# Softmax sums of two attentions in four column groups of the tensor engine, reciprocals spread by DMA

## The reference

```python
logits = einsum('bqhgd,bkhd->bhgqk', qg, k) * scale      # layer 0: 4 key heads, rotary
w = softmax(where(causal, logits, -1e30), axis=-1)
out = einsum('bhgqk,bkhd->bqhgd', w, v)                  # layer 1: the same with 16 key heads
```

## Time and profile before

| what | value |
|---|---|
| median of 3 runs | 1986.06 us (1983.82 to 1986.65) |
| time of the profiled execution | 1981.67 us |
| its span, first to last instruction | 1979.9 us |
| busy: PE / DVE / ACT / POOL | 1832.5 / 1336.2 / 958.2 / 1239.3 us |
| attention of layer 0, about | 45 to 529 us of the span |
| attention of layer 1, about | 690 to 1150 us of the span |
| mean granted clock of TensorE | 0.967 |
| DMA | 155.96 MB, 134304 packets on SP's queue |

### The profile page before, as it was taken

The page is one execution under the profiler, slowest core; times in us unless marked ns, Lnnn a source line. Parts: engine busy times, 40 slices in busy tenths (PEclk is TensorE's granted clock), DMA queues, the critical chain, the costliest instruction groups (busy, mean ns, idle before and its releaser), DMA issues.

```text
span 1979.9 us, 31923 instructions
## 1 busy us (share of the span) xinstructions
PE 1832.5 (93%) x10080; PEld 1273.4 (64%) x10080; DVE 1336.2 (67%) x3765; ACT 958.2 (48%) x2008; POOL 1239.3 (63%) x1454
## 2 busy tenths in 40 slices
PE   5999999999896899999999999999889999988985
PEld 4566666666595566676766567787556666655564
DVE  8899888888344866666667446556677787764633
ACT  2544445455455455554555534546344545544543
POOL 1766788888654467767777710011367888789953
PEclk8999999999998899999999999999789999999997
DMA  5224243232153343543444220000313233323243
GB/s 151 68 66 114 65 104 92 71 70 62 48 180 92 89 102 76 117 93 86 102 95 98 66 89 22 1 13 1 85 41 72 61 72 78 71 67 85 62 126 97
DMA packets 138569, 155.96 MB, mean 79 GB/s; under 512 B 34480, under 2 KB 78800, under 8 KB 138144
## 3 DMA queue, kind: packets, MB, share of 16 engines
q1 hardware_dynamic: 134304, 145.80, 30.0%
q0 software_dynamic: 4096, 8.12, 1.3%
HBM read 47.96 MB, written 17.52 MB: 33 GB/s over the span
## 4 chain that ended last, share of the span: by engine, by line
PE 61%; DVE 13%; POOL 10%; issue 6%; ACT 3%; SPq 3%; DMA 3%; POOLq 0%; DVEq 0%; ACTq 0%
PE P L904 60%; POOL acc L1707 3%; POOL yd L1730 3%; DVE mx L2118 3%; SPq L1834 2%; DMA qA<-hq 2%; DVE P L2129 2%; POOL xg L1721 1%; POOL acc L1704 1%; POOL pr L1685 1%; ACT pr L1450 1%; PE P L1003 1%; POOL z L1713 1%; PE P L942 0%; DVE mx L2129 0%
## 5 line engine op out<-in xcount | busy, mean ns | idle before, releaser
L1707 POOL TENSOR_TENSOR acc<-acc,pr 128x512 f32<-128x512 f32 (+5 forms) x640 | 659.8, 1050 | 43.1 <-ACT pr L1450 18.2
L1450 ACT ACTIVATE pr<-P 128x512 f32<-128x512 f32 (+1 forms) x768 | 396.8, 568 | 327.9 <-PE P L904 285.1
L904 PE MATMUL P<-pr,vt 128*64 128x512 f32 (+3 forms) x2304 | 403.4, 491 | 5.0 <-POOL pr L1685 4.8
L904 PE MATMUL P<-qA,kA 128*128 128x512 f32 (+2 forms) x1024 | 389.1, 383 | 13.9 <-ACT pr L1450 13.1
L904 PE MATMUL P<-qB,kB 128*128 128x512 f32 (+2 forms) x1024 | 368.0, 365 | 0.0
L904 PE MATMUL P<-kA,qA 128*128 128x512 f32 (+2 forms) x1152 | 316.8, 377 | 32.8 <-DMA qA<-hq 11.5
L1685 POOL TENSOR_SCALAR_AFFINE_SELECT pr<-pr 128x256 f32<-128x256 f32 x384 | 156.7, 409 | 277.1 <-ACT pr L1450 218.4
L904 PEld LDWEIGHTS P<-pr,vt 128*64 128x64 f32 x2304 | 154.4, 137 | 226.3 <-issue 189.7
L2118 DVE TENSOR_REDUCE mx<-P 128x1 f32<-128x512 f32 x384 | 243.7, 684 | 35.9 <-PE P L904 33.8
L904 PEld LDWEIGHTS P<-kA,qA 128*128 128x128 f32 x1152 | 193.9, 196 | 98.6 <-issue 24.3
L904 PEld LDWEIGHTS P<-qA,kA 128*128 128x128 f32 x1024 | 195.1, 191 | 90.9 <-ACT pr L1450 45.6
(11 more groups left out here) (355 smaller groups left out, 2842.0 us busy)
## 6 DMA issues: line engine op xcount, KB each, us to landing
qA<-hq SPq DMA_DIRECT2D x384, 128.0 KB, 2.4
kA<-stage SPq DMA_DIRECT2D x158, 128.0 KB
qB<-qB SPq DMA_DIRECT2D x96, 128.0 KB, 2.4
kB<-stage SPq DMA_DIRECT2D x79, 128.0 KB
rb<-sum_share SPq DMA_DIRECT2D x60, 128.0 KB, 2.9
yd<-in_c_zero SPq DMA_DIRECT2D x32, 128.0 KB, 2.7
w<-in_L_W SPq DMA_DIRECT2D x16, 256.0 KB, 5.0
xg<-xg SPq DMA_DIRECT2D x24, 129.0 KB
```

The lines of the kernel that those rows point to most:

```text
L904: return P.matmul(out, lhs, rhs, start=start, stop=stop)
L1450: S.activation(a.pr[slot][:, r, 512 - wide:512], m.bank[b][:, 512 - wide:512], AF.Exp, scale=0.125).then_inc(s.free[b], 1)
L1707: G.tensor_tensor(acc[:, :, sl], acc[:, :, sl], pt[:, :, sl], ALU.add).then_inc(s.acc, 1)
```

## The change

In layers 0 and 1:

- `C` is four matmuls of 32 output columns over 256 queries: group g (rows 32g to 32g+31) holds head g // 2, queries 256 (g % 2) and on.
- `yinv` works on 128 x 256 and no longer waits for the D of the chunk before but for its widening transfers.
- A new step `N` (newt, VectorE): the Newton step on 128 x 256, two instructions; it frees the bank of the sum.
- A new step `Y` (widen, SP): waits for N, for the widening transfers of the chunk before and for the output projection that read `z` last; then it issues four DMAs, each of which copies one row of `rd` (1 KB) onto 64 rows of `z`.
- `D` is one instruction, `z = pv * z` on 128 x 512; it waits for the four transfers.
- The orders of layers 0 and 1 are written anew.

```diff
-                if kind in HELD and len(got) == n - 1 and (kind != "close" or at_once(*item[1:4])):
-                    self.held[b] = (HELD[kind],) + item[1:]
+                    self.held[b] = ("newt" if kind == "close" and item[1] != 3 else HELD[kind],) + item[1:]
...
 STEPS = {
-    0: ("k0 S q0 k0' R1 S q1 q0' S S C1 k0\" q1' q0\" D1 q1\" V1 k1 + S M2 S M0 k1' S v1 M4 + S M1 C0 V + k1\" + "
-        "D0 R0 M6 S + M5 O0 M8 S v0 O1 M3 S S M7 V2 + + M9"),
-    1: ("S + + q0 q0' S k0 R1 k0' S S + q1 k0\" C1 q0\" D1 q1' + q1\" V1 S v0 S M1 M0 S O1 v1 M2 + S M5 M3 + S + "
-        "k1' k1 M6 S C0 + V1 k1\" + R0 D0 + M4 S M7 + S + V4 M8 O0 M9 + +"),
+    0: ("k0 S q0 k0' R1 S q1 q0' S C1 S V1 k0\" N1 Y1 q1' q0\" q1\" k1 M2 + S D1 M0 k1' S v1 S + M4 S M1 C0 V + k1\" + N0 Y0 R0 M6 S M5 + D0 M8 S O0 v0 O1 M3 S S M7 V2 + + M9"),
+    1: ("S + q0' q0 + S k0 R1 k0' S S q1 k0\" C1 q0\" N1 Y1 + q1' + q1\" V1 S M0 v0 M1 D1 S S O1 M2 v1 + S M5 M3 + S + k1' k1 M6 C0 + k1\" S V1 + + Y0 R0 N0 M4 S M7 D0 V4 + S + M8 O0 M9 +"),
...
+        elif kind in ("newt", "widen"):
+            if L != 3:
+                od.add(kind, *done)
...
-                if at_once(*k[0:3]):
+                if L == 3 and at_once(*k[0:3]):
                     for r in range(2):
                         t = mm(ps[64 * r:64 * r + 64, :], m.ones[:], acc[:, r, :], True, True)
...
-                if old and at_once(*old[0:3]):
+                if old and L != 3:
+                    w.wait_ge(s.widen, 64 * od.nth("widen", *old))
+                elif old and at_once(*old[0:3]):
...
-                own.mark(S.activation(a.rd[:], m.bank[b][:], AF.Ln))
+                cols = slice(0, 512 if L == 3 else 256)
+                own.mark(S.activation(a.rd[:, cols], m.bank[b][:, cols], AF.Ln))
                 own.settle()
-                S.activation(a.rd[:], a.rd[:], AF.Exp, scale=-1.0).then_inc(s.inv, 1)
+                S.activation(a.rd[:, cols], a.rd[:, cols], AF.Exp, scale=-1.0).then_inc(s.inv, 1)
...
+            elif kind == "widen":
+                a, old = m.A[k[0]], pl.put_out(*k)
+                z = a.z[pl.chunk(*k) % 4]
+                w.wait_ge(*pl.emptied("close", *k))
+                w.wait_ge(s.widen, 64 * od.nth("widen", *k) - 64)
+                if old:
+                    w.wait_ge(*pl.filled("out", *old))
+                for g in range(4):
+                    Y.dma_start(z[64 * (g // 2):64 * (g // 2) + 64, 256 * (g % 2):256 * (g % 2) + 256],
+                                a.rd[32 * g:32 * g + 1, 0:256].unsqueeze(1).broadcast_to([1, 64, 256])).then_inc(s.widen, 16)
...
+            elif kind == "newt":
+                y = m.A[k[0]].rd[:, 0:256]
+                b, _, _ = od.bank[("close",) + k][0]
+                sums = m.bank[b][:, 0:256]
+                w.wait_ge(s.inv, od.nth("yinv", *k))
+                chain(V.scalar_tensor_tensor(out=sums, in0=sums, scalar=-1.0, in1=y, op0=ALU.mult, op1=ALU.mult))
+                V.scalar_tensor_tensor(out=y, in0=sums, scalar=2.0, in1=y, op0=ALU.add, op1=ALU.mult).then_inc(s.free[b], 1)
+            elif kind == "div" and k[0] != 3:
+                z = m.A[k[0]].z[pl.chunk(*k) % 4]
+                b, _, _ = od.bank[("pv",) + k + (0,)][0]
+                w.wait_ge(s.pv, od.nth("pv", *k, kts(k[0], k[3])[-1]))
+                w.wait_ge(s.widen, 64 * od.nth("widen", *k))
+                V.tensor_tensor(z[:], m.bank[b][:], z[:], ALU.mult).then_inc(s.free[b], 1)
```

More of the change, by code:

```diff
@@ L201 @@
 SCORED = [(0, kt) for kt in range(4)] + [(1, kt) for kt in range(8)]
-SHARES_OUT = {"C": "close", "F": "fold", "I": "recip", "W": "spread", "B": "cast", "Z": "zraw", "D": "div", "O": "out"}
+SHARES_OUT = {"C": "close", "F": "fold", "I": "recip", "W": "spread", "B": "cast", "Z": "zraw", "N": "newt", "Y": "widen", "D": "div", "O": "out"}
 STEPS = {
-    0: ("k0 S q0 k0' R1 S q1 q0' S S C1 k0\" q1' q0\" D1 q1\" V1 k1 + S M2 S M0 k1' S v1 M4 + S M1 C0 V + k1\" + "
-        "D0 R0 M6 S + M5 O0 M8 S v0 O1 M3 S S M7 V2 + + M9"),
-    1: ("S + + q0 q0' S k0 R1 k0' S S + q1 k0\" C1 q0\" D1 q1' + q1\" V1 S v0 S M1 M0 S O1 v1 M2 + S M5 M3 + S + "
-        "k1' k1 M6 S C0 + V1 k1\" + R0 D0 + M4 S M7 + S + V4 M8 O0 M9 + +"),
-    3: ("q0 + k0' + k0 k1 q0' k0\" S V3 + R1 S q0\" + v0 C1 S S + M1 M0 F1 k1' S q1' q1 S + + W1 Z1 q1\" M2 I1 + "
-        "B1 + S v1 k1\" + V4 + M5 S O0' + D1 M3 S F0 X0 M6 C0 + R0 + W0 M4 S M9 V4 I0 Z0 + + M8 S M7 S X1 D0 "
-        "O1 B0")}
+    0: ("k0 S q0 k0' R1 S q1 q0' S C1 S V1 k0\" N1 Y1 q1' q0\" q1\" k1 M2 + S D1 M0 k1' S v1 S + M4 S M1 C0 V + k1\" + N0 Y0 R0 M6 S M5 + D0 M8 S O0 v0 O1 M3 S S M7 V2 + + M9"),
+    1: ("S + q0' q0 + S k0 R1 k0' S S q1 k0\" C1 q0\" N1 Y1 + q1' + q1\" V1 S M0 v0 M1 D1 S S O1 M2 v1 + S M5 M3 + S + k1' k1 M6 C0 + k1\" S V1 + + Y0 R0 N0 M4 S M7 D0 V4 + S + M8 O0 + M9 +"),
+    3: ("q0 + k0' + k0 k1 q0' k0\" S V3 + R1 S q0\" + v0 C1 S S + M1 M0 F1 k1' S q1' q1 S + + W1 Z1 q1\" M2 I1 + B1 + S v1 k1\" + V4 + M5 S O0' + D1 M3 S F0 X0 M6 C0 + R0 + W0 M4 S M9 V4 I0 Z0 + + M8 S M7 S X1 D0 O1 B0")}
 def project(L, kind, b, p, c):
@@ L743, in signals @@
     s.q_hi, s.k_hi, s.inv, s.recip, s.div = one("q_hi"), one("k_hi"), one("inv"), one("recip"), one("div")
-    s.fold, s.spread, s.cast = one("fold"), one("spread"), one("cast")
+    s.fold, s.spread, s.cast, s.widen = one("fold"), one("spread"), one("cast"), one("widen")
     s.rt_wh, s.rt_exp, s.xs, s.c_act, s.silu = one("rt_wh"), one("rt_exp"), one("xs"), one("c_act"), one("silu")
```

## The result

| | before | after |
|---|---|---|
| median of 3 runs | 1986.06 us | 2436.72 us (2434.48 to 2436.89) |
| span of the profiled execution | 1979.9 us | 2435.1 us |
| mean granted clock of TensorE | 0.967 | 0.897 |
| first close to last close, layer 0 | 469.9 us | 674.8 us |
| first close to last close, layer 1 | 468.2 us | 703.7 us |

The kernel is slower by 450.7 us: the ratio is 1.2288, with a 95% interval of 1.2262 to 1.2314. The last two lines of the table come from the timelines of PE, from the first to the last start of `P<-acc,ones` in a layer. Layers 0 and 1 carry 440 of the 450 us.

A forecast was written before the change was run, and what follows sets the result against it. PE's list bounds both attentions. Layer 0 +10.5, layer 1 +15, first and last jobs' closes -2, ends +5: +28.5 on the profiled 1981.67 gives 2010.2; the median lies 4.4 higher, 2014 us. Range 1968 to 2110.

The forecast's parts named there:

- The sign: Whole kernel: slower by more than the 4 us a measurement can tell, chance 0.7.
- the landing of the one-row transfers: Layers 0 and 1, Y's four copies: landing taken as 2.4 us, with 2.9 and 5.3 as other readings.
- slow rows: Rival: one-row transfers land at 5.3 us, delaying M4, M5 and D0's reader; 2143 us; chance 0.2.
- The closes: PE in layers 0 and 1: each close falls from 0.91 to 0.57 us, gaining 0.34 on each of 64.
- the odd jobs: Layer 1: Y1 adds 2.4 us before M5, less 0.34 for C0; C1's gain is lost in the wait.
- The orders: Layer 0, first half of a job: one filler outside a gap and one gap empty, +0.44 us.
- The push of q1's copies: SP's queue: Y1's four issues, 2.4 us, delay q1's copies; +10.5 us in layer 0, +15 in layer 1, closes included.
- the ends: End of each attention, last chunk uncovered: issues and landing add 4.2, shorter work saves 1.9; +2.3 twice, +5 us.
- ScalarE and VectorE: Layers 0 and 1: Ln and exp fall from 0.60 to 0.37 us, Newton from 0.70 to 0.42, covered by PE.
- D0's cover: VectorE: D0 stands late enough for its transfers; in layer 0 about 8.3 us after C0, with no wait for O0.

The follow-up runs named there:

- e9: Changed kernel in exactly the orders of before, without the widening transfers, D multiplying by other data of the same size: 1961.02 us, ratio 0.9883.
- e4: Changed kernel with its new orders, without the widening transfers, D multiplying by another tile: 2013.33 us, ratio 1.012.
- e1: Changed kernel with each widening transfer reading 32 equal rows twice instead of one row 64 times: 2065.76 us, ratio 1.0388.
- e12: Changed kernel with each widening transfer reading one row of memory (an input) instead of a row of SBUF, same place and waits: 2069.35 us.
- e7: e1 with nearly the old orders, Y1 behind q1's copies, and in layer 0 Y0 behind R0 and D0 ahead of M5: 2113.73 us, ratio 1.0636.
- e8: e1 with Y1 placed behind q1's copies in both layers, otherwise the new orders: 2105.8 us, ratio 1.0599.
- e2: Changed kernel with each widening transfer reading four adjacent rows 16 times each instead of one row 64 times: 2616.43 us.

## Why the prediction was wrong

The sign was right and the size was not: the time lies far above the range. Four steps account for it, each the difference of two medians:

| step | by | us |
|---|---|---|
| closes, shorter reciprocals, N | e9 against before | -23 |
| new orders | e4 against e9 | +52 |
| transfers, spread source | e1 against e4 | +52 |
| one row as source | after against e1 | +371 |

**The failing step is the landing of the one-row transfers.** I bounded it by 2.4, 2.9 and 5.3 us and took 2.4, "by `qA<-hq`". It measured 6.0 (the median of 256), above my upper bound, and 9.8 for the four of a chunk. With the source alone changed (e1) 371 of the 451 us are gone. My rival slow rows had the mechanism, with M4 behind the queue and D on VectorE, but priced it by the 5.3 of the earlier trace rows: 2143 us. I had argued against it with `rb<-sum_share`, which reads memory; e12 shows that memory rows say nothing about SBUF rows. The Trainium skill's SBUF — State Buffer (Door 1: The DMA port swizzle) stood beside the rival, with an estimate of 9.6 us for the four of a chunk and a kernel beyond 2300. The trace has 9.8 us and 2437, and that warning deserved more than the 0.2 that I gave the rival. But the 9.6 took the four transfers one after another at the rate of one port; the page's table puts their rows behind two ports, and the 9.8 holds the time from issue to first byte too. That the two numbers lie so close is in part luck.

No term of mine, the rival's included, held the clock: I priced PE's waits alone, and behind them its busy time grew by 132 us over the two layers.

**The closes** came out as priced in the medians, 23 us by e9 against 22, and that is partly luck: in the profiled executions the two layers give 14 us, all of it in layer 0. In layer 1 I had the odd jobs lose the gain of C1 alone; with e9, where nothing is pushed, none of it is to be seen. Each close takes 0.57 us, also where V with its 64 columns follows, as in this job of e7:

```profile
424.57 0.64 PE L900 MATMUL P<-acc,ones 128*32 128x256 f32 x8
425.14 1.30 PE L900 MATMUL P<-pr,vt 128*64 128x128 f32 x8
```

The Trainium skill's TensorEngine Tiling (Key Properties) says that a change of tiling mode drains the engine. The trace agrees so far as the 0.1 us that I would have gained without a drain isn't there; a drain by itself shows in no row.

**The orders** are the second error. I charged the new orders with 0.44 us a job in layer 0, 6 us in all, and with nothing in layer 1. They cost 52 (e4 against e9). The mechanism of the 0.44 was right (two score tiles side by side, PE waiting for exp), but I worked it out at one place of one layer.

**The push of q1's copies** was right in kind: in e1 four issues of 2.52 us stand ahead of q1's. With the landings and the ends I had some 40 us for the transfers (10 in layer 0, 22 in layer 1, 8 for the ends, before what the shorter instructions save), and e1 against e4 gives 52. Taking the push away (e8) moves the wait to D instead.

**ScalarE and VectorE** came out as priced: 0.385 and 0.43 us, where I had 0.37 and 0.42. I had called D0's cover sufficient in both layers and not priced D1's at all. In the kernel after D waits in all 64 chunks, and in e1, with its fast transfers, it still does in 39, for 68 us in all.

Nor would the forecast of 2014 have fitted the kernel with its source spread: e1 is at 2066. Orders and transfers cost 104 us there, where my sum had some 46. That the kernel without any transfers takes 2013 is chance.

## What to carry to other kernels

Before a DMA reads one row of SBUF many times, don't price it by a copy of the same size from many rows, nor by one that reads a row of memory; look for a row of the trace with such a source, or measure one. If the data stand in several rows, spread the reading over rows that lie apart: eight apart was fast here, neighbours were not. A slow transfer costs more than its own reader: price what is behind it in its queue and behind its reader on the engine. And before a kernel whose bounding engine is full gets a new order, price every place where a filler goes away, and try the order by itself with the new part left out.

## What the runs showed of the hardware

- Reading one row of SBUF many times: 256 KB, from one row for each 64 KB, took 9.8 us from first issue to last landing, and slowed copies from other rows queued behind it (four issues 6.33 us instead of 2.4). Four neighbouring rows were slower still (2616 against 2437 us), four rows eight apart fast (2079), and so were 32 rows (2066) and one row of memory (2069).
- The issue instruction itself is held when the transfers ahead of it are slow: the four `z<-rd` issues took 2.52 us in e1, 3.45 in the kernel after and 6.24 in e2.
- TensorE's granted clock was 1.00 in both attentions before (2.4 GHz throughout) and 0.87 and 0.86 after, where PE waits for up to 10 us at a time and is at 1.2 GHz for part of the time behind the waits. Behind the wait of 5.77 us, from 416.40 to 421.00, the granted clock is 0.50, and the two matmuls of M4 take 1.22 us; those of the earlier trace rows with no wait ahead take 0.62 and 0.63. So PE's busy time from first to last close rose with less work to do, from 455 to 514 us in layer 0 and from 461 to 534 in layer 1.
